# Output projection of an adaLN block: one product of 512 columns for both weight parts, its second range added by ScalarE and GpSimd

## The reference

```python
mod = (_silu(L0_c) @ L0_wmod).reshape(L0_c.shape[0], 6, 1, -1)
sa, ca, ga, sb, cb, gb = (mod[:, 0], mod[:, 1], mod[:, 2], mod[:, 3], mod[:, 4], mod[:, 5])
h = _layernorm(x, axis=-1) * (1 + ca) + sa
x = x + ga * _L0_attn_ref(h, L0_attn_query_proj, L0_attn_key_proj, L0_attn_value_proj, L0_attn_output_proj)
h = _layernorm(x, axis=-1) * (1 + cb) + sb
x = x + gb * _L0_ffn_ref(h, L0_ffn_w_gate, L0_ffn_w_up, L0_ffn_w_down)
```

```python
xq = fp4_quant_dequant(x); wq = fp4_quant_dequant(w)
gate = fp4_linear(x, w_gate); y = fp4_linear(x, w_up); h = silu(gate) * y; fp4_linear(h, w_down)
```

## Time and profile before

| | us |
|---|---|
| median of 3 runs | 1687.57 |
| lowest and highest | 1687.49, 1687.82 |
| the profiled execution | 1687.39 |
| its span, first to last instruction | 1686.1 |
| PE busy | 1639.9 (97%) |
| DVE busy | 1580.5 (94%) |
| ACT busy | 1374.2 (82%) |
| POOL busy | 777.2 (46%) |
| granted clock of PE, mean | 0.998 |

### The profile page before, as it was taken

The page is one execution under the profiler, slowest core; times in us unless marked ns, Lnnn a source line. Parts: engine busy times, 40 slices in busy tenths (PEclk is TensorE's granted clock), DMA queues, the critical chain, the costliest instruction groups (busy, mean ns, idle before and its releaser), DMA issues.

```text
span 1686.1 us, 38834 instructions
## 1 busy us (share of the span) xinstructions
PE 1639.9 (97%) x15446; PEld 814.2 (48%) x15446; DVE 1580.5 (94%) x1708; ACT 1374.2 (82%) x2508; POOL 777.2 (46%) x1625
## 2 busy tenths in 40 slices
PE   8999999999999999999999999999999999999998
PEld 7743233333333333673333333333333379999997
DVE  7899999999999999769999999999999879988887
ACT  5499999999999999669999999999999833333332
POOL 3034445454444445303444544566654457555542
PEclk9999999999999999999999999999999999999999
DMA  6102111112111112511111121111112533534420
GB/s 233 64 8 71 52 50 45 45 45 71 51 51 52 46 45 76 163 43 44 46 46 45 45 69 51 51 52 46 46 45 63 157 114 126 155 125 152 148 67 19
DMA packets 83103, 123.15 MB, mean 73 GB/s; under 512 B 4706, under 2 KB 69098, under 8 KB 82922
## 3 DMA queue, kind: packets, MB, share of 16 engines
q1 hardware_dynamic: 82506, 120.15, 22.4%
q10 hardware_dynamic: 416, 0.53, 0.1%
HBM read 74.52 MB, written 46.15 MB: 72 GB/s over the span
## 4 chain that ended last, share of the span: by engine, by line
DVE 63%; PE 32%; ACT 2%; issue 2%; POOL 1%; DMA 0%; ACTq 0%; POOLq 0%; DVEq 0%
DVE nm L1073 60%; PE acc L443 13%; PE slot L443 10%; PE acc L610 6%; PE slot L666 1%; PE slot L581 1%; DVE ost L1086 1%; ACT e_sb L820 1%; PE slot L464 0%; DMA v_sb<-in_wmod 0%; PE acc L641 0%; DVE qs L1140 0%; DVE e_sb L1128 0%; ACT e_sb L749 0%; DVE e_sb L1147 0%
## 5 line engine op out<-in xcount | busy, mean ns | idle before, releaser
L1073 DVE TENSOR_REDUCE nm<-slot 128x1 f32<-128x1024 f32 x1024 | 1166.1, 1213 | 20.6 <-PE slot L581 18.5
L820 ACT ACTIVATE e_sb<-slot,nm 128x1024 f32<-128x1024 f32 x1024 | 1136.9, 1112 | 17.5 <-DVE nm L1073 12.6
L610 PE MATMUL acc<-e_sb,vp 64*64 64x512 f32 x8192 | 1060.9, 594 | 6.3 <-DVE ost L1086 4.7
L581 PE MATMUL slot<-stq,stk 64*64 64x512 f16 x4096 | 411.5, 388 | 21.6 <-ACT e_sb L820 21.6
L581 PEld LDWEIGHTS slot<-stq,stk 64*64 64x64 f16 x4096 | 117.6, 103 | 625.8 <-ACT e_sb L820 592.1
L610 PEld LDWEIGHTS acc<-e_sb,vp 64*64 64x64 f32 x8192 | 283.3, 132 | 188.6 <-issue 74.0
L1308 POOL TENSOR_TENSOR dlt<-nm 128x4 f32<-128x4 f32 x128 | 25.6, 200 | 412.1 <-DVE nm L1073 412.1
L820 ACT ACTIVATION_READ_ACCUMULATOR e_sb<-slot,nm 128x1 f32 x1024 | 199.8, 195 | 0.0
L1299 POOL TENSOR_TENSOR vp<-v_sb,fac 128x512 f32<-128x512 f32 x128 | 133.4, 1042 | 10.2 <-POOL fac L1289 0.3
L1285 POOL TENSOR_TENSOR rtot<-tot,mone 128x4 f32<-128x4 f32 x128 | 132.7, 1037 | 10.0
L1279 POOL TENSOR_TENSOR wsum<-cor,ssum 128x8 f32<-128x8 f32 x128 | 25.9, 202 | 234.2 <-ACT cor L850 234.2
(11 more groups left out here) (179 smaller groups left out, 1926.8 us busy)
## 6 DMA issues: line engine op xcount, KB each, us to landing
o_r<-o_heads SPq DMA_DIRECT2D x32, 1024.0 KB, 7.5
stk<-qk_parts SPq DMA_DIRECT2D x128, 128.0 KB
o_heads<-ost_hi SPq DMA_DIRECT2D x64, 256.0 KB, 3.4
o_heads<-ost SPq DMA_DIRECT2D x64, 256.0 KB, 4.1
v_sb<-in_x SPq DMA_DIRECT2D x16, 512.0 KB, 6.5
qk_parts<-e_sb SPq DMA_DIRECT2D x32, 256.0 KB, 2.4
stq<-qk_parts SPq DMA_DIRECT2D x128, 64.0 KB
out<-e_sb SPq DMA_DIRECT2D x32, 128.0 KB, 1.8
```

The source lines that it names most:

```text
L581: mm = pe.matmul(slot[s][side * VD:(side + 1) * VD, c * 512:(c + 1) * 512], stk[c * 64:c * 64 + 64, h % 2, i * P + side * VD:i * P + (side ...
L610: mm = pe.matmul(acc[half * VD:(half + 1) * VD, c * 512:(c + 1) * 512], vp[rows, g % 3, gi, half, :], e_v[rows, j % ERING, n0:n0 + 512], s ...
L820: act.activation(e_v[:, j % ERING, half * 1024:(half + 1) * 1024], slot[u % 3][:, :], ACT.Exp, bias=nm[:, g % 4, i, half:half + 1], accum_ ...
L1073: dve.tensor_reduce(nm[:, g % 4, i, half:half + 1], slot[u % 3][:, :], AX.X, ALU.max, negate=True).then_inc(maxed.sem)
```

## The change

For each chunk of the projection, one product of 512 columns multiplies the high part of the outputs with both weight parts, which now lie side by side (`wo_both`), and writes 512 columns of PSUM. A second product of 256 columns adds low outputs times high weights to the first 256 columns. So there are two ranges, D = 256 columns each, to be added. For tiles 0 and 1 VectorE adds the second range to the residual's input first, in an instruction of its own. From tile 2 on ScalarE copies the second range to SBUF (`take_part`), GpSimd adds the copy to the input (`add_part`), and VectorE's sum waits for that. On VectorE the snaps now come before `token_moments`. GpSimd's folding writes the parts to their new places, with the chunks of batch 1 in reverse order.

```diff
-            products(proj[i], [(o_r[:, u % 2, 1, c, r * P:(r + 1) * P], o_r[:, u % 2, 0, c, r * P:(r + 1) * P],
-                                wo_lo[b][:, c, :], wo_hi[b][:, c, :]) for c in range(8)]).then_inc(proj_mm.sem)
+            for c in range(8):
+                pe.matmul(proj[i], o_r[:, u % 2, 0, c, r * P:(r + 1) * P], wo_both[b][:, c, :], start=(c == 0), stop=False)
+                mm = pe.matmul(proj[i][:, 0:D], o_r[:, u % 2, 1, c, r * P:(r + 1) * P], wo_both[b][:, c, 0:D],
+                               start=False, stop=(c == 7))
+            mm.then_inc(proj_mm.sem)
...
+        def take_part(i):
+
+            act.wait_ge(*proj_mm.past(i))
+            if i >= 3:
+                act.wait_ge(*part_added.past(i - 3))
+            act.copy(part2, proj[i][:, D:2 * D]).then_inc(part_taken.sem)
...
             act.wait_ge(*attended.past(B * JT - 1))
+            take_part(2)
...
                     take_h(i - 4)
+                if i + 1 < TILES:
+                    take_part(i + 1)
                 if i <= TILES + 2:
                     square(i)
...
-            dve.wait_ge(*proj_mm.past(i))
-            if r == 0:
+            xi = xi_r[q % 2][:, r, :]
+            if i < 2:
+                dve.wait_ge(*proj_mm.past(i))
                 dve.wait_ge(*x_in[q % 2].past(q // 2))
-            dve.tensor_tensor(x2, xi_r[q % 2][:, r, :], proj[i], ALU.add).then_inc(x2_made.sem)
+                settle(dve.tensor_tensor(xi, xi, proj[i][:, D:2 * D], ALU.add))
+            else:
+                dve.wait_ge(*part_added.past(i - 2))
+            dve.tensor_tensor(x2, xi, proj[i][:, 0:D], ALU.add).then_inc(x2_made.sem)
...
+                if i <= TILES + 2:
+                    mix_snap(i)
                 if i + 1 < TILES:
                     token_moments(i + 1)
-                if i <= TILES + 2:
-                    mix_snap(i)
...
+        def add_part(i):
+
+            q, r = divmod(i, GROUP)
+            pool.wait_ge(*part_taken.past(i - 2))
+            if r == 0:
+                pool.wait_ge(*x_in[q % 2].past(q // 2))
+            xi = xi_r[q % 2][:, r, :]
+            pool.tensor_tensor(xi, xi, part2, ALU.add).then_inc(part_added.sem)
...
             pool.wait_ge(*attended.past(B * JT - 1))
+            add_part(2)
             inverse_root2(2)
             for i in range(2, TILES + 3):
                 if i < TILES:
                     spread_input(i)
+                if i + 1 < TILES:
+                    add_part(i + 1)
                 scale_mix(i)
```

More of the change, by code:

```diff
@@ L212, in adaln_block @@
         wo_x = place("wo_x", [P, 8, D], WV_AT)
-        wo_hi = [upper[:, :, 0:D], place("wo_hi1", [P, 8, D], WV_AT, F32R)]
-        wo_lo = [upper[:, :, D:2 * D], place("wo_lo1", [P, 8, D], WO_AT, F32R)]
+        wo_both = [upper[:, :, 0:2 * D], place("wo_both1", [P, 8, 2 * D], WO_AT, F32R)]
+        wo_low1 = place("wo_low1", [P, 8, 2 * D], WO_AT)[:, :, D:2 * D]
         wgu_hi = [place(f"wgu_hi{k}", [P, 2 * F], ST_AT + k * 1408 * 4, F32R) for k in range(2)]
@@ L228, in adaln_block @@
         outb = region(e_sb, 10080, 3, D)
+        part2 = region(e_sb, 6880, D)
         xqT_lo = place("xqT_lo", [P, 2, 2, P], E_AT + 6368 * 4, F32R)
@@ L235, in adaln_block @@
         tp = slot[2]
-        proj = [slot[i][:, 0:D] for i in range(3)] + [acc[:, 0:D]] * (TILES - 3)
+        proj = [slot[i][:, 0:2 * D] for i in range(3)] + [acc[:, 0:2 * D]] * (TILES - 3)
         def down_at(i):
@@ L290, in adaln_block @@
         gate_mm, up_mm, h_turned, down_mm = tally("gate_mm"), tally("up_mm"), tally("h_turned"), tally("down_mm")
-        rstd2_made = tally("rstd2_made")
+        rstd2_made, part_taken, part_added = tally("rstd2_made"), tally("part_taken"), tally("part_added")
         uses, last_uses = bank_uses()
@@ L1233, in fold_wo @@
                 pool.wait_ge(*got_rows.past(0))
-            w = wo_s if b else wo_x
+            if b:
+                c = 7 - c
+            w = wo_low1 if b else wo_x
             sem, n = pool_own.next()
@@ L1238, in fold_wo @@
             sem, n = pool_own.next()
-            pool.tensor_copy(wo_hi[b][:, c, :], w[:, c, :]).then_inc(sem)
+            pool.tensor_copy(wo_both[b][:, c, 0:D], w[:, c, :]).then_inc(sem)
             pool.wait_ge(sem, n)
-            low(pool, wo_lo[b][:, c, :], w[:, c, :], wo_hi[b][:, c, :]).then_inc(wo_split.sem)
+            low(pool, wo_both[b][:, c, D:2 * D], w[:, c, :], wo_both[b][:, c, 0:D]).then_inc(wo_split.sem)
         def split_head(b, h, p):
```

## The result

| | median, us | lowest to highest | runs |
|---|---|---|---|
| before | 1686.96 | 1683.86 to 1690.85 | 22 |
| the change | 1690.89 | 1687.46 to 1693.79 | 22 |

The ratio is 1.0023, 95% interval 1.0017 to 1.0029: the change costs 3.9 us (2.9 to 4.9). The forecast was 1689.2 us, +0.1%, with a range of 1685.0 to 1693.5. The time lies in the range, and the side is that of my sum. The size is not: +1.6 us was forecast against +3.9, and the ratio stands just over the 0.2% up to which I had called it no change.

What follows compares the result with a forecast made beforehand. PE was taken to bound the stage after attention. Plain tiles -2.1, splitting tiles +2.3, start +0.6, iteration 16 +0.2 and end +0.6 made +1.6 us on 1687.57: 1689.2 us, range 1685.0 to 1693.5.

Steps and rivals of the forecast that it cites:

- The bound, and the path of a plain tile: Middle of the stage: PE bounds the tiles, the new path to the snap hides, a plain tile goes to 9.66 us.
- T: Time origin within a tile: the start of its first transposing product on PE, from which the forecast counts.
- The projection: PE, each tile: 8 x 0.227 + 8 x 0.120 = 2.77 us, saving 0.106; 20 plain tiles give -2.1 us.
- The last sentence of the prediction: PE: a 512-column product not taking 0.227 us, with weights changing and half its columns added again, would break the sum.
- The splitting tiles: Iterations 5 to 8, GpSimd splitting the last head: PE waits for the scaling, period 10.1, then 10.4 in three; +2.3 us.
- As GpSimd starts each further one later: Splitting tiles: the period grows from 10.1 in the first to 10.4 in three more, 0.33 + 3 x 0.65 = +2.3 us.
- The start: First tiles: later sum, low part behind GpSimd's scaling, gate_up(2) at about 1386.3 instead of 1385.84; +0.6 us.
- Iteration 16: Second weight split: wdb's low part stands behind the statistics and the scaling ends 0.2 us later; +0.2 us.
- The end: From 1645.81: first hidden product at T+8.43 instead of T+7.81, behind snap and statistics; +0.6 us.
- 1: Plain tiles: GpSimd wins the port tie against VectorE, gate_up waits, 9.77 us a tile; 1692.0 us, 17%.
- 2: Plain tiles: ring of projection, copy, square, snap, scaling, turn_h becomes the bound, period 9.98 us; 1695.6 us, 8%.
- 3, the clock: Start: PE idles some 2.4 us before gate_up(2), its clock falls, costing 1.5 us; 1690.7 us, 16%.

Runs made afterwards that it cites:

- e3_wide_then_narrow: The changed kernel with the eight products of 512 columns ahead of the eight of 256, instead of in turns: 1690.06 us, ratio 1.0028.
- e4_before_turns: The kernel before plus 16 transposing products that nothing reads, where PE waits at the start: 1685.49 us, ratio 0.9992.
- e8_order_alone: The kernel before with only the new VectorE order, snaps ahead of the sum (token_moments): 1686.13 us, ratio 0.9999.
- e1_vector_adds: The changed kernel with VectorE adding both ranges in every tile, without ScalarE's copy and GpSimd's addition: 1685.90 us, ratio 0.9997.
- e10: The changed kernel with the old VectorE order, sum ahead of the snaps: 1710.91 us (four executions), ratio 1.0147.
- e12: The changed kernel with ScalarE's square ahead of its copy, old order for iterations 2 and 3, and 16 unread transposing products at the start: 1686.04 us, 0.9995.
- e2_square_first: The changed kernel with ScalarE's square ahead of its copy of the second range: 1686.47 us, ratio 0.9997.
- e6_change_again: The changed kernel itself, measured once more with nothing altered: 1690.07 us, ratio 1.0022 to before.
- e9: The changed kernel, VectorE adding both ranges, wide products first, old order up to iteration 3, unread transposing products at the start: 1683.73 us, ratio 0.9983.
- e7: The changed kernel, VectorE adding both ranges, wide products first, unread transposing products at the start and ahead of gate_up(2) and gate_up(15): 1685.99 us, 0.9995.
- e5: The changed kernel plus unread transposing products ahead of turn_x(2), turn_h(0) (8 each) and gate_up(2) (18): 1689.43 us, ratio 1.0019.

## Why the prediction was right, and where its steps were off

**The bound, and the path of a plain tile: right.** Tiles are all PE; the copy starts at T+3.89 (1483.56, with T at 1479.67), forecast 3.85, VectorE waits for the square, the sum on GpSimd ends 0.12 us before the snap (forecast 0.1), and the scaling and low_x hide.

**The projection: mechanism right, size wrong.** Forecast 2.77 us and 0.106 saved; measured 2.83 and 0.054. The step that failed is "8 x 0.227 + 8 x 0.120": the 0.227 of the earlier trace rows is of 12 wide products in a row. In a row e3_wide_then_narrow has 0.230; next to a narrow one it is 0.235. The last sentence of the prediction names this as what would break the sum. By the rule of the Trainium skill ("TensorE: Matmul & The Clock Gate", "Back-to-back issue gap") for isolated products, the columns at 2.4 GHz plus about 2.5 ns, an estimate of a pair is 0.325 us; the trace has 0.354, so the rule is off on both shapes here. Over 20 tiles the term is -1.1 and not -2.1.

**The splitting tiles: mechanism right, +2.3 is too much.** GpSimd's sum and the snaps do meet at the port, and PE does wait for the scaling, as forecast. But the four tiles take 9.98, 9.92, 9.92 and 9.93 us. Against the 9.76 from which the +2.3 was counted that is +0.7 in all (+0.9 over 9.71), and the delay doesn't grow. A held snap took 0.42 to 0.47 us more, not 0.65, and as GpSimd's sum gives way to the first snap in three of the four it doesn't start later each time. "As GpSimd starts each further one later" was argued and not read from a row. The forecast's own 10.1 is a little high too: T+10.25 less T+9.88 on top of 9.66 is 10.03. That the port is shared is in both traces; the Trainium skill ("SBUF — State Buffer", "SBUF: two separate sides") tells of an exclusive lock, and the 1.66 and 1.58 us for operations of 0.74 and 1.16 agree with it.

**The start: +0.6 forecast, +1.2 between the profiles, +2.7 in truth.** The parts were all named: the sum later (1.0 us forecast, 1.2 measured, from the first projection), the low part behind GpSimd's scaling (2.73 us now), gate_up(2) behind VectorE. The step that failed is taking the 4.37 us of the projection in the earlier trace rows for a cost of before that the change saves. It was a clock fall that before has in some executions: e4_before_turns has the start at 38.52. From it to the change it is 2.69 us. Step by step, the new order adds 0.96 (e8_order_alone), the wide products with the second add on VectorE 0.29 (39.77 of e1_vector_adds less 39.48), and the copy with GpSimd's sum the other 1.44. These shares hold for this sequence only: with the copy and GpSimd's sum in place, the old order has 41.41 and 41.95 (e10, e12), so there it gives nothing back.

**Iteration 16: +0.2 forecast, +0.07 measured, and the sum of two large things.** The order alone takes 1.56 us out; the copy ahead of the square puts 1.3 of it back (21.95 against 20.66 in e2_square_first). I had seen neither, so the small error here is luck.

**The end: +0.6 forecast, +0.64 measured** (45.00 against 44.36), by the step given: snap and statistics ahead of the hidden product. e2_square_first, in which the snap doesn't wait, has 44.36 again.

**The rivals.** 1 didn't happen: VectorE was 0.02 us ahead and won. 2 didn't happen; e10_change_old_order shows that a ring of this kind binds as soon as the sum stands ahead of the snaps. 3, the clock, was given 16% and 1690.7; the profile of the change has no fall, that of the same kernel in e6_change_again has two. It is a matter of the execution, not of the kernel alone. (The wait at iteration 16 that I gave as 2.1 us is 1.88 us in before's timeline.) The median of +3.9 is the 3.1 of the path without falls, and what is left is within the interval. At equal mean clock the change costs 2.9 to 3.5 us, so falls are a small part of it at most.

**All together, against e4_before_turns:** start +2.7, the 12 tiles with the splitting ones +0.35, iteration 16 +0.1, the 12 plain tiles -0.6, end +0.6: +3.1. That my +1.6 is as near as it is has luck in it. Measured less forecast it is +1.0 for the projection, -1.6 for the splitting tiles, +2.1 for the start and -0.1 for iteration 16, and errors of both signs partly cancelled.

## What to carry to other kernels

Where a new hand-over between engines is put ahead of work that others wait for, its place in the queue matters more than its length: a copy of 0.37 us, moved from ahead of its neighbour to behind it, gave back 2.9 us (342.1 against 340.7 less a fall of 1.5). Before a long time in a profile is booked as a cost that a change removes, see the granted clock beside it: if the clock had fallen, it may not be there in the next execution. And a step that moves work past a shared port is to be priced at each place by itself; in the kernel before, the same reordering lost 1.0 us at the start and won 1.6 in iteration 16 and the next.

## What the runs showed of the hardware that I had not expected

**The same wait, with and without a fall.** Two executions of the same kernel, the changed one; busy time by stretch (engines, then granted clock, DMA share, GB/s), first the profile of the change, then e6_change_again:

```profile
1380.50:1383.00 2.50, 2.27 (x14) 1.71 (x12) 2.43 (x4) 1.37 (x3) 1.71 (x5) 1.00 0.00 0
1383.00:1385.00 2.00, 0.00 (x0) 0.00 (x0) 1.93 (x4) 0.31 (x2) 0.05 (x2) 1.00 0.00 0
1385.00:1387.00 2.00, 1.76 (x11) 1.76 (x12) 2.00 (x3) 0.89 (x1) 1.43 (x2) 1.00 0.00 0
```

```profile
1383.00:1385.00 2.00, 0.04 (x1) 0.04 (x1) 1.97 (x4) 0.40 (x1) 0.29 (x1) 1.00 0.00 0
1385.00:1387.00 2.00, 2.00 (x10) 2.00 (x11) 2.00 (x2) 0.61 (x1) 1.14 (x2) 0.79 0.00 0
1387.00:1389.00 2.00, 2.00 (x8) 2.00 (x8) 1.93 (x4) 0.76 (x1) 0.57 (x1) 0.50 0.03 8
```

Ahead of this gate_up PE idles 2.47 us in the one and 2.45 us in the other. In the one the granted clock stays at 1.00, 2.4 GHz; in the other it goes to 0.50, 1.2 GHz, when PE is busy again. The other profiles say the same. Over all of them, of nine waits of 2.41 to 2.48 us ahead of a gate_up, five were followed by a fall (in e1, e2, e3, e6 and e9) and four not (in the change, e8, and at the end of e1 and e7). Of four waits of 2.27 to 2.29 us at iteration 16, two were (e3, e6) and two not (the change, e5). No run here shows what decides between them.

**Wide products next to narrow ones** take 0.235 us, in a row 0.230; narrow ones 0.119.
